# The first four tiles: output-projection and key blocks interleaved over six PSUM banks, K/V/R weights fetched two groups ahead, first tile reordered

## The chip, the cores and the metric

One Trainium2 chip, all 8 cores. Each core runs the same program on one batch row of 8192 tokens; no core waits for another. The metric is the device time of the slowest core in microseconds. The engines of a core are TensorE (PE; its weight loads are listed as PEld), VectorE (DVE), ScalarE (ACT), GpSimd (POOL) and SyncE (SP). POOL and SP only issue transfers here; every engine works through its own list of instructions in order and waits on semaphores.

## The reference

One layer: an RWKV block (time mixing, then channel mixing) beside a feed-forward block with ternary weights, on the same normalized input.

```python
xn = _layernorm(x)                                   # over 1024 features
# RWKV block on xn
h  = _ln(xn); h1 = _time_shift(h)
k, v, r = mix(h, h1, tm_mix_*) @ tm_Wk, tm_Wv, tm_Wr # three 1024x1024 products
x1 = xn + (sigmoid(r) * _wkv(k, v, w, u)) @ Wo       # decay recurrence over time
h  = _ln(x1); h1 = _time_shift(h)
kc = square(relu(mix(h, h1, cm_mix_k) @ cm_Wk))      # 1024 -> 4096
rc = sigmoid(mix(h, h1, cm_mix_r) @ cm_Wr)
x2 = x1 + rc * (kc @ cm_Wv)                          # 4096 -> 1024
# feed-forward block on xn
f  = gelu(xn @ ternary(W1).T + b1) @ ternary(W2).T + b2
return x + x2 + f
```

## The kernel before

**Layout.** Features lie on the partitions (8 chunks of 128), tokens on the free axis, in 16 tiles of 512 tokens. A "block" is one output chunk of one product: eight 128x128 by 128x512 matmuls into one PSUM bank (`block`, L326). All matrix work is such blocks; two more blocks with a matrix of ones give the sums of a normalization.

**Order.** The program is written out by Python into one list per engine (`Streams.put`, L47, which also drops waits that the engine has already passed). The feed-forward part of a tile runs four tiles later (`LAG`): the loop at L910 over tiles 0 to 3 has attention and channel mixing only, since the ternary weights are being made meanwhile; the loop at L947 over the other tiles has both. The change edits the first loop, what lies ahead of it, and a few helpers.

In a tile t of the first loop TensorE does, in this order: the eight output-projection blocks (`wo_stage`, L746), two blocks of sums (`ln2_stats`), for t above 0 the last five chunks of the value product of tile t-1 (`value_part`, 20 blocks), and then `channel_stage` (L861): 32 key blocks, the receptance blocks and the first three value chunks (all eight in tile 3). Between these blocks `between()` counts n and puts in one K/V/R group of tile t+1 (`kvr_group`, L578: three blocks into banks 5, 6 and 7) every 5 blocks from n = 16 in tile 0, every 5 from n = 11 in tiles 1 and 2, every 7 from n = 11 in tile 3.

**The rest is in lanes.** `Lanes` (L64) holds Python generators, each step of which emits a few DVE or ACT instructions with an estimated cost. `advance`, called after each block, gives 0.93 of the block's 1740 ns to the lanes in order of priority; `drain` emits all that is left of a lane at once. The lanes are `wkv` (the recurrence of one group, priority 1), `ln2_apply` (second normalization and mixing of this tile, pair by pair of chunks into xk2 and xr2, priority 0), `ln0_stats`, `ln0_mix` and `ln0_norm` (first normalizations of the next tile, its mixing into xk, xv and xr, and its store to memory). `ln0_mix` stops while `mixer["hold"]` is set, which `ln2_stats` sets after its two blocks, and `ln2_apply` clears. A K/V/R group of tile t+1 needs the whole `ln0_mix(t+1)`, an output-projection block the whole att, a key block the whole xk2.

**Evictions.** A key block is evicted by ACT in two instructions (Relu at L796, Square at L798) from banks 2, 3 and 4 in turn; output-projection blocks by DVE (L758) from banks 2 to 7.

**Weights.** In tile 0, and for some of the value rows in tile 1, they come as f32 through POOL with a conversion to bf16 (`prepare`, L280) into one of two slots of ring A (K/V/R rows), four of ring B or two of ring C, and SP writes each row back to memory (the z tensors) as soon as it has landed. From then on SP loads the bf16 rows (`fetch`). SP works in order: a load stands behind all write-backs issued before it. A slot is refilled when `release` is told the last matmul that read it. From tile 1 a paced lane (`tern_run`) also reads W1 and W2 through POOL, sums and rounds them on ACT and clips them on DVE.

Of the kernel before, what the change touches and what calls it, by code (L numbers as in the profile page):

```python
# [15 lines left out]
E = 1024  # L16
# [112 lines left out]
def build_program(t_total=T_TOTAL):  # L129
# [207 lines left out]

    short = {"banks": [2, 3, 4, 5, 6, 7], "at": 0}
# [10 lines left out]
    def ln0_stats(j):  # L349
# [31 lines left out]
        for c in range(EC):  # L381
# [4 lines left out]
        a1 = ACT(lambda s_: s_.activation(out=R0[:], in_=pb[bk2][:], func=AF.Ln, scale=1.0 / E, bias=LN0_EPS),  # L386
                 t6, tk.get("ln0_done"), tk.get("norm_done"))
        a2 = ACT(lambda s_: s_.activation(out=R01[:], in_=pb[bk2][:], func=AF.Ln, scale=(1.0 + LN_EPS) / E,
                                          bias=LN0_EPS * LN_EPS))
        bank_free[bk2] = [a2]  # L390
        ACT(lambda s_: s_.activation(out=R0[:], in_=R0[:], func=AF.Exp, scale=-0.5), a1)
        tk[f"rstd{j}"] = ACT(lambda s_: s_.activation(out=R01[:], in_=R01[:], func=AF.Exp, scale=-0.5), a2)
# [67 lines left out]
    def ln0_norm(j):  # L460

        cur = xn[j % 2]
        for p in range(4):
            tn = DVE(lambda v, p=p: v.tensor_mul(pair(cur, p), pair(x, p), twice(R0)),
                     tk[f"rstd{j}"], tk.get(f"x2_free{j % 2}"))
# [14 lines left out]
    def ln2_apply(t, s1, s2, bk1, bk2):  # L480
# [14 lines left out]
        for p in range(5):  # L495
# [22 lines left out]
    def wkv(t, g, kb, vb, rb, ktok, vtok, rtok):  # L518
# [47 lines left out]
        def last():  # L566
            wk["nd_free"] = tk["att"] = DVE(lambda v: v.tensor_mul(ck(att, g), ND[:, 0, :], ND[:, 1, :]), l2,  # L567
# [10 lines left out]
    def kvr_group(t, g):  # L578
        unit = fetch("wkvr", g)
        if t == 1 and g + 1 < EC:  # L580
            prefetch("wkvr", g + 1)
# [8 lines left out]
        release(unit, toks[-1])  # L590
        tk["kvr_done"] = toks[-1]
# [154 lines left out]
    def wo_stage(t):  # L746
        short["banks"], short["at"] = [2, 3, 4, 5, 6, 7], 0
        cur = xn[t % 2]
        unit = None
        ev = None  # L750
        for c in range(EC):
            if c % 2 == 0:
                unit = fetch("wo", c // 2)
            bk = short_bank()
            tok = block(bk, unit[0], (c % 2) * 1024, [ck(att, k) for k in range(8)], True, True, unit[1], tk["att"])
# [4 lines left out]
            if c % 2:  # L760
# [3 lines left out]
                    ev, tk.get("w1_done"), tk.get("cwk_done"))  # L764
            ln.advance(BLOCK_NS, 750.0)
# [23 lines left out]

    def cwk_block(m, unit):  # L790
        bk = short_bank()
        tok = block(bk, unit[0], (m % 2) * 1024, [ck(xk2, k) for k in range(8)], True, True, unit[1], tk["mix2"])
        if m % 2:
            release(unit, tok)
        i = m % 2
# [65 lines left out]
    def channel_stage(t, chunks, first, every, hooks):  # L861
# [12 lines left out]
        for m in range(FC):  # L874
# [25 lines left out]
    for g in range(EC):  # L900
# [4 lines left out]
        if g == 4:  # L905
            lane_s = ln.start(3, ln0_stats(1))
    refill(rC)


    for t in range(LAG):  # L910
        ln.drain(wkv_lanes[-1])
        ln.drain(lane_s)
# [5 lines left out]
        ev, s = wo_stage(t)  # L918
# [11 lines left out]
        def mixed(t=t, lane=mix_lanes[0]):  # L930
            if t == 0:
                prefetch("wkvr", 0)
# [10 lines left out]
        gates = channel_stage(t, range(EC if t == LAG - 1 else EC - LATE), first, every, hooks)  # L943
# [155 lines left out]
```

How the kernel before makes its waits and increments, by code:

```python
            def body(eng):  # L981
                for ws, fn, sem, by in st.ops[name]:
                    for s, v in ws:
                        eng.wait_ge(sems[s], v)
                    ins = fn(eng)
                    if sem is not None:
                        ins.then_inc(sems[sem], by)
```

## Time and profile before

| | us |
|---|---|
| median of 3 runs | 5135.28 |
| lowest, highest | 5126.62, 5996.21 |
| the profiled execution | 5128.33 |
| span of its slowest core (core 0, the one shown) | 5126.5 |
| spans of its other cores | 5105.4 to 5123.9 |
| TensorE busy | 4776.4 (93%) |
| VectorE, ScalarE busy | 2595.4, 2131.2 |

The highest of the three runs lies 17% above the others. All rows below are of core 0 of the profiled execution, and their times count from its first instruction.

### The profile page before, as it was taken

The page shows a single profiled execution, that of the slowest core. Times are in us where ns is not written, and L with a number is a line of the kernel's source. Part 1 is how long each engine was busy: PE and PEld are TensorE (multiplying, and loading weights), DVE is VectorE, ACT ScalarE, POOL GpSimd, SP SyncE. Part 2 cuts the span into 40 slices and gives each one's busy share as a digit, 9 for nine tenths or more (in the row PEclk, how much of TensorE's full clock was granted, in tenths as well). Part 3 has the DMA queues.
Part 4 walks back from the last instruction along what each step waited for, and adds up shares of the span by engine and source line. Part 5 has one row for each costly group of instructions (what it writes and reads, how often), then busy time and mean ns, then how long its engine had stood idle before and what let it go on. Part 6 is the DMA issues. An engine that isn't in the chain of part 4 may idle for free.

```text
span 5126.5 us, 63290 instructions; the slowest of 8 cores (5105.4 to 5126.5 us)
## 1 busy us (share of the span) xinstructions
PE 4776.4 (93%) x21484; PEld 2154.9 (42%) x21922; DVE 2595.4 (51%) x3424; ACT 2131.2 (42%) x3436; POOL 429.7 (8%) x807
## 2 busy tenths in 40 slices
PE   3577888799999999999999999999999999999999
PEld 1233333344444444444444444444444444444444
DVE  6746566666555545555554555545555554330111
ACT  2433756554544434354443435444343544342111
POOL 0000111122000000100000010000001000000111
PEclk8789999899999999999999999999999999999999
DMA  6477878899455564645556464555646455555765
GB/s 159 103 193 180 261 230 244 249 291 318 165 189 199 177 225 160 231 158 192 202 179 216 163 230 163 192 190 196 202 166 226 159 185 192 175 185 189 230 227 179
DMA packets 273339, 1021.40 MB, mean 199 GB/s; under 512 B 34432, under 2 KB 34560, under 8 KB 267008
## 3 DMA queue, kind: packets, MB, share of 16 engines
q1 hardware_dynamic: 194112, 706.83, 40.6%
q0 software_dynamic: 78768, 310.43, 20.7%
q8 instruction: 183, 3.00, 0.2%
q14 instruction: 132, 1.08, 0.1%
q10 hardware_dynamic: 144, 0.07, 0.0%
HBM read 916.52 MB, written 127.93 MB: 204 GB/s over the span
## 4 chain that ended last, share of the span: by engine, by line
PE 84%; DMA 7%; DVE 4%; issue 2%; ACT 2%; POOL 0%; another core or an unknown queue 0%; DVEq 0%; SPq 0%; ACTq 0%; POOLq 0%
PE pb L333 82%; DMA rb<-w2t 2%; DMA rb<-w1t 1%; DMA ra<-zwkvr 1%; PE pb L382 1%; PE pb L775 1%; DMA rb<-cwk 1%; DMA zw2t<-XC 1%; PE pb L779 1%; DVE xr L419 1%; DVE TT L414 0%; DMA x<-xS 0%; DVE xk L419 0%; DMA rb<-cwv 0%; ACT TT L376 0%
## 5 line engine op out<-in xcount | busy, mean ns | idle before, releaser
L333 PE MATMUL pb<-xk,rb 128*128 128x512 bf16 x8028 | 1785.6, 381 | 81.5 <-DVE xr L419 60.0
L333 PE MATMUL pb<-big,rb 128*128 128x512 bf16 x8034 | 1792.3, 379 | 16.9 <-DMA rb<-cwv 5.7
L333 PEld LDWEIGHTS pb<-xk,rb 128*128 128x128 bf16 x8192 | 802.7, 98 | 1051.9 <-issue 96.5
L333 PEld LDWEIGHTS pb<-big,rb 128*128 128x128 bf16 x8192 | 801.9, 98 | 979.2 <-issue 16.4
L796 ACT ACTIVATE RC<-pb 128x512 f32<-128x512 f32 x512 | 301.4, 589 | 725.5 <-PE pb L333 640.3
L703 ACT ACTIVATE big<-pb,vecs_s 128x512 bf16<-128x512 f32 x512 | 346.3, 686 | 563.9 <-PE pb L333 550.3
L735 DVE SCALAR_TENSOR_TENSOR RO<-pb,vecs_s,RO 128x512 f32<-128x512 f32 x128 | 95.9, 749 | 580.3 <-PE pb L333 386.2
L333 PE MATMUL pb<-xk,ra 128*128 128x512 bf16 x1005 | 255.6, 396 | 109.9 <-DMA ra<-zwkvr 44.8
L525 DVE TENSOR_TENSOR_SCAN W<-wdec,carry,pb 128x512 f32<-128x512 f32 x128 | 163.7, 1279 | 361.4 <-PE pb L333 361.4
L798 ACT ACTIVATE big<-RC 128x512 bf16<-128x512 f32 x512 | 322.5, 630 | 47.5 <-ACT RC L796 0.8
L838 DVE TENSOR_TENSOR RO<-pb,RC 128x512 f32<-128x512 f32 x113 | 77.9, 690 | 478.1 <-PE pb L333 478.1
L758 DVE TENSOR_TENSOR xn<-xn,pb 128x512 bf16<-128x512 bf16 x128 | 87.6, 687 | 411.2 <-PE pb L333 362.7
L406 ACT ACTIVATE hp<-TT,vecs_s 128x512 bf16<-128x512 f32 x256 | 194.4, 809 | 163.6 <-DVE TT L501 148.0
L333 PE MATMUL pb<-att,rb 128*128 128x512 bf16 x1006 | 227.5, 384 | 37.0 <-DVE att L567 34.8
L333 PE MATMUL pb<-xr,rc 128*128 128x512 bf16 x997 | 243.6, 385 | 15.2 <-DMA rc<-cwr 7.6
L814 ACT ACTIVATE RC<-pb 128x512 f32<-128x512 f32 x128 | 76.2, 595 | 421.3 <-PE pb L333 363.6
L333 PE MATMUL pb<-xv,ra 128*128 128x512 bf16 x1000 | 244.4, 385 | 4.8 <-DVE W L543 3.9
L543 DVE TENSOR_TENSOR W<-W,pb 128x512 f32<-128x512 f32 x128 | 88.0, 687 | 317.6 <-ACT W L536 310.9
L333 PE MATMUL pb<-xr,ra 128*128 128x512 bf16 x1001 | 240.2, 379 | 1.4
L536 ACT ACTIVATE W<-W 128x1024 f32<-128x1024 f32 x128 | 134.1, 1048 | 174.7 <-DVE W L533 174.7
L333 PEld LDWEIGHTS pb<-xk,ra 128*128 128x128 bf16 x1024 | 102.0, 100 | 241.2 <-issue 130.1
L419 DVE SCALAR_TENSOR_TENSOR xk<-TT,vecs_s,hp 128x512 bf16<-128x512 f32 x256 | 182.0, 747 | 11.9 <-DVE TT L414 0.9
(102 smaller groups left out, 3875.6 us busy)
## 6 DMA issues: line engine op xcount, KB each, us to landing
rb<-zw1t SPq DMA_DIRECT2D x256, 512.0 KB, 3.7
rb<-zw2t SPq DMA_DIRECT2D x256, 512.0 KB, 5.0
rb<-zcwk SPq DMA_DIRECT2D x240, 512.0 KB, 4.9
rb<-zcwv SPq DMA_DIRECT2D x240, 512.0 KB, 6.0
ra<-zwkvr SPq DMA_DIRECT2D x120, 768.0 KB, 7.2
resS<-RO POOLq DMA_DIRECT2D x128, 256.0 KB, 5.7
rb<-w1t POOLq DMA_DIRECT2D x64, 512.0 KB, 8.9
rb<-w2t POOLq DMA_DIRECT2D x64, 512.0 KB, 10.1
```

The costliest lines, as they stand in the source:

```text
L333: tok = PE(lambda t, k=k: t.matmul(pb[bank][:], slot[:, col + k * 128:col + (k + 1) * 128], rhs[k], start=start and k == 0, stop=stop and ...
L406: a1 = ACT(lambda s, c=c: s.activation(out=h[:, c, 1:NT + 1], in_=src[:, c, :], func=AF.Identity, scale=cv[gname][:, 2 * p + c:2 * p + c + 1],
L419: m = DVE(lambda v, c=c, mname=mname, dst=dst: v.scalar_tensor_tensor(out=ck(dst, 2 * p + c), in0=tc[:, c, :], scalar=cv[mname][:, 2 * p + ...
L525: p = DVE(lambda v: v.tensor_tensor_scan(out=W4[:, 0, now], data0=w_b, data1=pb[kb][:], initial=carry[:, g, 0:1], op0=ALU.add, op1=ALU.max ...
L536: ex = ACT(lambda s: s.activation(out=W4[:, 2:4, now], in_=W4[:, 2:4, now], func=AF.Exp), d0, d1)
L543: bv = DVE(lambda v: v.tensor_mul(W4[:, 1, now], W4[:, 2, now], pb[vb][:]), ex, vtok)
L703: gel[m] = ACT(lambda s, m=m, bk=bk: s.activation(out=ck(big, m), in_=pb[bk][:], func=AF.Gelu, bias=cv["b1f"][:, m:m + 1]), tok, *big_free ...
L735: e1 = DVE(lambda v, r=r, c=c, bk=bk: v.scalar_tensor_tensor(out=RO[r][:], in0=pb[bk][:], scalar=cv["b2f"][:, c:c + 1], in1=RO[r][:], op0= ...
L758: ev = DVE(lambda v, c=c, bk=bk: v.tensor_add(ck(cur, c), ck(cur, c), pb[bk][:]), tok, xn_st[t])
L796: a1 = ACT(lambda s, i=i, bk=bk: s.activation(out=RC[i][:], in_=pb[bk][:], func=AF.Relu), tok, rl_free[i])
L798: sqr[m] = ACT(lambda s, i=i, m=m: s.activation(out=ck(big, m), in_=RC[i][:], func=AF.Square), a1, *big_free[m // 8])
L838: e1 = DVE(lambda v, r=r: v.tensor_mul(RO[r][:], pb[bk][:], gate), tok, a3, ro_free[r])
```

## The change

It touches only what the first loop and the code ahead of it emit, but for one swap in `ln0_stats` that every tile has.

```diff
@@ prepare: every f32 row load also waits for the first tile's x
-        ready = dma("gpsimd", f"G{ring.name}{i}", slot[:], wdram[w][rows, :], *ring.free[i])
+        ready = dma("gpsimd", f"G{ring.name}{i}", slot[:], wdram[w][rows, :], *ring.free[i], *x_in[0])
@@ new
+    def rounds(jobs, parts):
+
+        done = {}
+        for at, (ks, ready) in enumerate(parts):
+            for bank, slot, col, rhs, loaded in jobs:
+                for k in ks:
+                    w = [ready] if k == ks[0] else []
+                    if at == 0 and k == ks[0]:
+                        w += [loaded, *bank_free[bank]]
+                    tok = PE(lambda t, bank=bank, slot=slot, col=col, rhs=rhs, k=k: t.matmul(
+                        pb[bank][:], slot[:, col + k * 128:col + (k + 1) * 128], rhs[k], start=k == 0, stop=k == 7),
+                        w, inc=k == 7)
+                done[bank] = tok
+        return done
@@ ln0_stats: R01 (for mixing) complete first, then R0 (for the store), each with its own token
+        for r, key, scale, eps in ((R01, "rstd", (1.0 + LN_EPS) / E, LN0_EPS * LN_EPS), (R0, "rstd0", 1.0 / E, LN0_EPS)):
...
@@ ln0_norm
+        while f"rstd0{j}" not in tk:
+            yield -2000.0
@@ ln2_apply, after the mixing of each pair
+                tk[f"mix2_{pend[3]}"] = tk["mixed"]
@@ wkv: one token for each group's slice of att
-            wk["nd_free"] = tk["att"] = DVE(lambda v: v.tensor_mul(ck(att, g), ND[:, 0, :], ND[:, 1, :]), l2,
+            wk["nd_free"] = tk[f"att{g}"] = DVE(lambda v: v.tensor_mul(ck(att, g), ND[:, 0, :], ND[:, 1, :]), l2,
@@ kvr_group
-        if t == 1 and g + 1 < EC:
-            prefetch("wkvr", g + 1)
...
         release(unit, toks[-1])
+        if t == 1 and g + 2 < EC:
+            prefetch("wkvr", g + 2)
@@ wo_stage(t, split): six blocks side by side, k 0 to 6 once att6 is there, k 7 with att7
+        if split:
+            for r in range(3):
+                units[r] = fetch("wo", r)
+            early = rounds([(2 + c, units[c // 2][0], (c % 2) * 1024, rhs, units[c // 2][1]) for c in range(6)],
+                           [(range(7), tk["att6"]), ((7,), tk["att7"])])
...
+            if split and c == 3:
+                mixer["hold"] = True
@@ new: the first six key blocks, two k's of each as each pair of xk2 is there
+    def cwk_first():
+
+        units = [fetch("cwk", r) for r in range(3)]
+        done = rounds([(2 + m, units[m // 2][0], (m % 2) * 1024, [ck(xk2, k) for k in range(8)], units[m // 2][1])
+                       for m in range(6)], [((2 * p, 2 * p + 1), tk[f"mix2_{p}"]) for p in range(4)])
+        for m in range(6):
+            if m % 2:
+                release(units[m // 2], done[2 + m])
+            cwk_evict(m, 2 + m, done[2 + m])
@@ channel_stage(..., split)
-        for m in range(FC):
+        if split:
+            cwk_first()
+            n = 6
+        for m in range(n, FC):
@@ ahead of the first loop
-        if g == 4:
-            lane_s = ln.start(3, ln0_stats(1))
     refill(rC)
+    prefetch("wkvr", 0)
+    prefetch("wkvr", 1)
@@ the first loop
-        ln.drain(lane_s)
+        if t:
+            ln.drain(lane_s)
...
-        ev, s = wo_stage(t)
+        ev, s = wo_stage(t, True)
...
-            mix_lanes[:] = [ln.start(2, ln0_mix(t + 1))]
+            mix_lanes[:] = [ln.start(2, itertools.chain(ln0_stats(1), ln0_mix(1)))]
...
-        first, every = (16, 5) if t == 0 else (11, 5) if t < LAG - 1 else (11, 7)
...
-            if t == 0:
-                prefetch("wkvr", 0)
...
+        first, every = (16, 4) if t == 0 else (12, 4) if t < LAG - 1 else (12, 6)
```

The statistics of tile 1 thus move from between the K/V/R groups of tile 0 to behind the second normalization of tile 0. In the second loop `wo_stage` and `channel_stage` are called as before.

## Rows read from the trace of the kernel before

**Rows 1.** The page, parts 1 and 2: busy us (share) xinstructions; TensorE in 40 slices

```profile
PE 4776.4 (93%) x21484; PEld 2154.9 (42%) x21922; DVE 2595.4 (51%) x3424; ACT 2131.2 (42%) x3436; POOL 429.7 (8%) x807
...
PE   3577888799999999999999999999999999999999
```

**Rows 2.** Windows of core 0: stretch, length, busy us (instructions) by engine, granted clock, DMA share, GB/s

```profile
144.50:172.00 27.50, 5.17 (x12) 1.69 (x12) 17.36 (x20) 8.44 (x11) 0.00 (x0) 0.57 0.00 0
...
190.50:217.70 27.20, 0.00 (x0) 0.01 (x1) 25.84 (x30) 8.70 (x18) 0.00 (x0) 0.59 0.22 68
...
269.40:407.70 138.30, 112.75 (x480) 49.41 (x490) 69.83 (x94) 58.59 (x93) 10.60 (x20) 0.91 0.69 174
407.70:421.30 13.60, 0.00 (x0) 0.02 (x1) 10.46 (x15) 2.80 (x4) 0.54 (x1) 0.61 0.17 58
...
514.77:646.86 132.09, 118.89 (x520) 52.22 (x529) 78.23 (x106) 96.27 (x166) 15.34 (x29) 0.97 0.86 254
646.86:660.30 13.44, 0.00 (x0) 0.01 (x1) 4.05 (x8) 2.30 (x4) 2.67 (x5) 0.60 0.51 176
...
986.67:1152.66 165.99, 154.87 (x678) 68.33 (x692) 103.16 (x147) 95.13 (x134) 35.34 (x66) 0.97 0.91 282
1152.66:5126.50 3973.84, 3933.48 (x17911) 1789.48 (x18275) 1857.74 (x2440) 1565.75 (x2513) 290.32 (x542) 1.00 0.58 195
```

**Rows 3.** Timeline, VectorE, start: start, length, what, [idle before <-releaser]

```profile
23.23 1.23 DVE L354 TENSOR_TENSOR TT<-x 128x1024 f32<-128x1024 f32 x1 [12.66 <-DMA x<-xS]
```

**Rows 4.** Timeline, TensorE, first tile: statistics, and the first key block

```profile
160.10 2.04 PE L362 MATMUL pb<-TT,ones_f 128*128 128x512 f32 x2 [15.60 <-DVE TT L358]
...
217.72 3.15 PE L333 MATMUL pb<-xk,rb 128*128 128x512 bf16 x7 [27.23 <-DVE xr L419]
```

**Rows 5.** Timeline, VectorE, first tile: att slices of groups 6 and 7

```profile
146.60 0.68 DVE L567 TENSOR_TENSOR att<-ND 128x512 bf16<-128x512 f32 x1
...
154.87 0.69 DVE L567 TENSOR_TENSOR att<-ND 128x512 bf16<-128x512 f32 x1 [1.54 <-ACT ND L564]
```

**Rows 6.** Timeline, SyncE queue, first tile: write-backs ahead of the first K/V/R load

```profile
181.21 82.14 SPq L232 DMA_DIRECT2D zcwk<-rb  x12
```

**Rows 7.** Timeline, TensorE, channel stage of the first tile: waits for weights

```profile
269.41 3.57 PE L333 MATMUL pb<-xk,ra 128*128 128x512 bf16 x8 [21.38 <-DMA ra<-zwkvr]
...
314.03 0.59 PE L333 MATMUL pb<-xk,ra 128*128 128x512 bf16 x1 [14.56 <-DMA ra<-zwkvr]
...
348.10 5.80 PE L333 MATMUL pb<-xr,rc 128*128 128x512 bf16 x16 [7.58 <-DMA rc<-cwr]
```

**Rows 8.** Timeline, VectorE: mixing for the second tile

```profile
234.99 1.42 DVE L419 SCALAR_TENSOR_TENSOR xk<-TT,vecs_s,hp 128x512 bf16<-128x512 f32 x2
...
241.43 1.41 DVE L419 SCALAR_TENSOR_TENSOR xk<-TT,vecs_s,hp 128x512 bf16<-128x512 f32 x2
...
250.20 1.41 DVE L419 SCALAR_TENSOR_TENSOR xr<-TT,vecs_s,hp 128x512 bf16<-128x512 f32 x2
```

**Rows 9.** Timeline, VectorE, around the second tile's second normalization

```profile
448.04 0.68 DVE L487 SCALAR_TENSOR_TENSOR R<-pb,R 128x512 f32<-128x512 f32 x1
...
484.66 0.69 DVE L838 TENSOR_TENSOR RO<-pb,GG 128x512 f32<-128x512 f32 x1 [4.87 <-remote]
...
490.90 1.41 DVE L419 SCALAR_TENSOR_TENSOR xr<-TT,vecs_s,hp 128x512 bf16<-128x512 f32 x2
```

**Rows 10.** Timeline, TensorE: K/V/R groups of tiles 2 and 4; key blocks of tile 3

```profile
514.77 1.89 PE L333 MATMUL pb<-xk,ra 128*128 128x512 bf16 x8
...
957.60 18.62 PE L333 MATMUL pb<-xk,rb 128*128 128x512 bf16 x71 [16.61 <-DVE xr L419]
...
986.67 3.57 PE L333 MATMUL pb<-xk,ra 128*128 128x512 bf16 x8 [6.38 <-DVE xr L419]
```

**Rows 11.** The page, part 5: evictions of the key blocks on ScalarE

```profile
L796 ACT ACTIVATE RC<-pb 128x512 f32<-128x512 f32 x512 | 301.4, 589 | 725.5 <-PE pb L333 640.3
...
L798 ACT ACTIVATE big<-RC 128x512 bf16<-128x512 f32 x512 | 322.5, 630 | 47.5 <-ACT RC L796 0.8
```

More of the change, by code:

```diff
@@ L1 @@
+import itertools
 import numpy as np
@@ L385, in ln0_stats @@
         tk["sq_free"] = t6
[L386 to L392, printed above, removed]
+        for r, key, scale, eps in ((R01, "rstd", (1.0 + LN_EPS) / E, LN0_EPS * LN_EPS), (R0, "rstd0", 1.0 / E, LN0_EPS)):
+            a1 = ACT(lambda s_, r=r, scale=scale, eps=eps: s_.activation(
+                out=r[:], in_=pb[bk2][:], func=AF.Ln, scale=scale, bias=eps),
+                t6, tk.get("ln0_done"), tk.get("norm_done"))
+            tk[f"{key}{j}"] = ACT(lambda s_, r=r: s_.activation(out=r[:], in_=r[:], func=AF.Exp, scale=-0.5), a1)
+        bank_free[bk2] = [a1]
     hp_free = [None, None]
@@ L744, in w2_stage, with wo_stage @@
             ln.advance(BLOCK_NS, 1550.0)
-    def wo_stage(t):
+    def wo_stage(t, split=False):
         short["banks"], short["at"] = [2, 3, 4, 5, 6, 7], 0
         cur = xn[t % 2]
-        unit = None
-        ev = None
+        rhs = [ck(att, k) for k in range(8)]
+        units, early = {}, {}
+        if split:
[3 more added lines that the diff above has]
+                           [(range(7), tk["att6"]), ((7,), tk["att7"])])
         for c in range(EC):
-            if c % 2 == 0:
-                unit = fetch("wo", c // 2)
+            if c % 2 == 0 and c // 2 not in units:
+                units[c // 2] = fetch("wo", c // 2)
+            unit = units[c // 2]
             bk = short_bank()
-            tok = block(bk, unit[0], (c % 2) * 1024, [ck(att, k) for k in range(8)], True, True, unit[1], tk["att"])
+            if c in (0, 1, 2, 3, 4, 5) and split:
+                tok = early[bk]
+            else:
+                tok = block(bk, unit[0], (c % 2) * 1024, rhs, True, True, unit[1], tk["att7"])
             if c % 2:
@@ L794, in cwk_block, with cwk_evict @@
             release(unit, tok)
+        cwk_evict(m, bk, tok)
+    def cwk_evict(m, bk, tok):
         i = m % 2
@@ L859, in value_part, with channel_stage @@
                 cwv_block(t, c, q, unit, rc)
-    def channel_stage(t, chunks, first, every, hooks):
+    def channel_stage(t, chunks, first, every, hooks, split=False):
         short["banks"], short["at"] = [2, 3, 4], 0
@@ L925, in build_program, with mixed @@
         if t == 0:
-            mix_lanes[:] = [ln.start(2, ln0_mix(t + 1))]
+            mix_lanes[:] = [ln.start(2, itertools.chain(ln0_stats(1), ln0_mix(1)))]
         lane_n = ln.start(2, ln0_norm(t + 1))
-        first, every = (16, 5) if t == 0 else (11, 5) if t < LAG - 1 else (11, 7)
-        def mixed(t=t, lane=mix_lanes[0]):
-            if t == 0:
-                prefetch("wkvr", 0)
+        first, every = (16, 4) if t == 0 else (12, 4) if t < LAG - 1 else (12, 6)
+        def mixed(lane=mix_lanes[0]):
             ln.drain(lane)
@@ L942, in build_program @@
         hooks = {first: mixed, first + 4: normed, first + 16: stats}
-        gates = channel_stage(t, range(EC if t == LAG - 1 else EC - LATE), first, every, hooks)
+        gates = channel_stage(t, range(EC if t == LAG - 1 else EC - LATE), first, every, hooks, True)
     finish_lanes()
```

2 lines of the change are left out of this document (1 added, 1 removed).

## The prediction

> **What bounds the kernel now.** I read the slices of the page first: TensorE is at nine tenths or more from the tenth slice on and well below it only in the first nine [rows 1]. Then the windows by stretch. From 1152.66 us to the end, 3973.84 us hold by my count of the code some 2280 blocks, 1.74 us a block, at clock 1.00 [rows 2]. That part is bound by TensorE, the change leaves its order alone, and I give it nothing. All there is to win lies ahead of 1152.66: of the 4776.4 us busy [rows 1] 842.9 lie there, so TensorE waits 310 us, and runs now and then at the lower of its two clocks.
>
> Where do these waits sit? In each of the four tiles the same ring closes: the K/V/R groups feed the recurrence on VectorE, the last slice of att frees the output projection, its result goes through normalization and mixing on VectorE, mixing frees the key blocks and the next K/V/R groups. The rows to look at are those in which TensorE does nothing at all: 27.2 us of the second normalization of tile 0, then 13.60 and 13.44 us before the output projections of tiles 1 and 2, and some 22 of the 27.5 us ahead of the projection of tile 0 [rows 2]. Beside them stand waits for weights in tile 0 of 21.38, 14.56 and 7.58 us [rows 7].
>
> **The change part by part.** Sums are made against the profiled execution, 5128.33 us for a span of 5126.5; the median of the runs shown is 7 us above it. E0, E1, E2 are the ends of the channel stages of tiles 0, 1 and 2, before at 407.7, 646.9 and 873.6.
>
> *Start.* The second half of the first x is added at 23.23, after 12.66 us of waiting for its transfer, which shares the engines with six converted weight rows [rows 3]. Held back, those rows leave it the engines. It can't start adding before 10.6, where the wait began; landing by 11.5 gives 12 us (bounds 10 and 12.7). The weights then land some 10 us later, but are read only after statistics and four pairs of mixing at 6.44 us each [rows 8]: nothing. The swap in the statistics frees mixing two ACT instructions of some 0.6 us sooner [by rows 11]: 1 us. Sum 13.
>
> *Tile 0, att to the sums.* Before, TensorE's K/V/R groups end at 144.5, tile 1's statistics take 15.60 us of waiting and more [rows 2, 4], att is whole at 155.56 [rows 5], and the second sum ends at 190.5. After, 42 matmuls (7 k of six banks) start with att6 at 147.3 [rows 5]; at 1.74/8 = 0.22 us each that is 9.1, plus some 2 at the low clock (eight matmuls after a wait took 3.57 us against 1.89 without one [rows 7, 10]): 158.5. Six matmuls on att7 and two blocks, 4.8, to 163.3; the last add, square and second sum, some 4.5: 168. Gain 22 (19 to 25).
>
> *Tile 0, key blocks against mixing.* The 27.2 us on VectorE stay. Only 12 of 48 matmuls are left behind the last pair instead of 48, 7.9 us less. But the next K/V/R group needs tile 1's mixing, and this now has the statistics ahead of it. From the end of the second mixing I count: sums on VectorE 4.5; the small matmul and the copy behind seven evictions of 0.59 + 0.63 [rows 11], to 10; four subtractions to 15; squares behind evictions to 21; sums and the two logarithms and exponentials to 26; three store steps fill the wait for the first pair, then four pairs at 6.44 apart [rows 8], to 55 to 58. Before, the group started 51.8 us after that point, 217.6 to 269.41 [rows 4, 7], held by its weights although mixing had ended at 251.6 [rows 8]. So the wait for weights goes and a wait for VectorE stands in its place: loss 5 (from a gain of 2 to a loss of 12). The 7.9 us are gone in it; TensorE idles some 28 us there.
>
> *Tile 0, the other groups.* The write-backs issued ahead of the first K/V/R loads hold SP's queue for 82.14 us [rows 6]. Two groups ahead, each load stands behind write-backs of rows that are needed before it anyway. Its new price, SP waiting for the last matmul of a group, holds up only write-backs and loads of later rows. I take 13 of the 14.56 us [rows 7] and leave the receptance wait of 7.58, whose two slots are as before; 0 if converted rows are late instead, 17 with everything. So E0 comes 13 + 22 - 5 + 13 = 43 us earlier.
>
> *Tile 1.* The groups every four blocks end six blocks sooner against the end of the stage, 10 us, and 9 us of matmuls run before the last slice of att: the 13.60 goes. Six blocks side by side also leave one add, not eight, behind the last, but the converted rows of the value part start later; I count 57.7 us from E0 to the end of the value part against 76.6 (407.7 to 484.3): gain 19. The hold moved to the fourth block takes two pairs of `ln0_mix` (until 448.04) out of the way of the normalization [rows 9]. The gap of 8.2 after the value part, up to the last pair at 492.3 [rows 9], is then filled. But all four pairs of tile 2's mixing now come behind it. ACT has twelve evictions of 1.22 us [rows 11], some five passes of the ternary sums and four pairs' scalings from 8 us on, which ends near 37, and the last pair's mixing 5 later: the first group starts 42 us after the value part, before 30.5 (484.3 to 514.77 [rows 10]): loss 11.5. The rest, 132.09 us before [rows 2], has one block less and fewer waits for evictions: 127. Sum 12.5.
>
> *Tile 2* is the same with value rows that arrive as bf16 before and after: 13.44 us of waiting goes [rows 2], less at the edges: 9.5.
>
> *Tile 3.* The part from E2 to the end of its value part takes 55.5 instead of 67.4: gain 12. From there (941.0) the first group came 45.7 us later, with 16.61 us of waiting for the normalization, then two pairs, the last waited for for 6.38 [rows 10]; with four pairs, but a normalization that starts 11 sooner and no clips emitted while a lane is drained, 48: loss 2 to 3. The rest, 165.99 [rows 2], falls to 161. Sum 14.
>
> Total 43 + 12.5 + 9.5 + 14 = 79, and 5128.3 - 79 = 5049; **I forecast 5050 us**, 1.6% under the median.
>
> *A rule against the change.* The bursts of twelve matmuls between pairs come after waits of some 4 us, and eight matmuls took 3.57 us after a wait [rows 7], so a burst may take 5 us and not 2.6. The Trainium skill (TensorE: Matmul & The Clock Gate, section HAM oscillation) says that bursts parted by waits each start at the low clock, and advises to keep one output's K tiles together; the trace agrees on the price of a start. By the rule the bursts before the last pair cost nothing, since TensorE is idle there anyway, and the last costs 2.6 us in tile 0, which the wait for mixing swallows: 0 in the sum. By it, too, each idle stretch that the change removes saves 1.7 us; I count that within the terms.
>
> **The rivals.**
>
> *A. Mixing is no new wait.* If VectorE and ACT run the four pairs beside the key blocks faster than counted, the losses of 5, 11.5, 11.5 and 2.5 vanish and the filled gaps count: the sum rises by 31 to 110, and to 180 if TensorE waited nowhere but for receptance weights. For it: VectorE is free a third of the time in these stretches, 78.23 of 132.09 us busy [rows 2]. Against: four pairs at 6.44 are 26 us, and they can't begin before the first two key evictions. Times 5018 and 4950; I give 0.24 to all gains above 100.
>
> *B. Transfers take over.* DMA engines are at 0.86 and 0.91 in the later stretches of tiles 1 and 3 [rows 2]. If the denser order only meets later rows, the 13 of tile 0 and some 5 to 8 in each other tile go: gain 40 to 50, 5083. Against: at 0.69 in tile 0 [rows 2] there is room. 0.19.
>
> *C. The early parts aren't early.* If att6 is multiplied only just before att7, or the pairs of the key input come together, the rounds save nothing. In tile 0, 10 us go; in the others the denser groups cover most: gain 65, 5063. Against: 7.6 us lie between the two slices [rows 5]. 0.07.
>
> *D. Slower, by the deferred mixing.* In tile 3 VectorE waits for ACT in front of each clip, and two pairs took from 957.6 to 986.67, 29 us [rows 10]. If all four pairs go at that pace in tiles 1 to 3, they end 57 us after the normalization. In tiles 1 and 2 that is 61 behind the value part, 30 later than before, against 24 won elsewhere: 6 lost each. In tile 3 it is 65 against 45.7, with 17 won: 2 lost. Tile 0's four pairs, stretched by 0.6, cost 16 of its 43, and the weights' 13 go too: 14 left. The sum is 0 there; beyond that pace each further microsecond a pair costs 16, and one gives 5144. Against: `drain` emits no clips, and tiles 0 and 1 have none. 0.06.
>
> **How the numbers follow.** Forecast (gain 55 to 100) 0.44, A 0.24, B 0.19, C 0.07, D 0.06. The range runs from 5005, inside A, to 5092, the weak end of B, where the bounds of the terms in tile 0 (together 25 either way) also end; it leaves out some 0.1 on each side. Its own range for the forecast is 5030 to 5073. A change of over 2% is 103 us, about what a measurement of this kernel can tell from none: faster is A but for its edge and a little of the forecast, 0.27; slower by over 2% is the far end of D, 0.02; 0.71 lies within.
>
> **What will show it.** In the trace after: the second addition near 11; no statistics between tile 0's groups; output-projection matmuls before the last att multiply in all four tiles; key matmuls in four bursts in tile 0; the first K/V/R group of each next tile waiting for the last mixing on VectorE (28 us in tile 0, some 15 in tiles 1 and 2) and not for weights; no wait of 13 us ahead of projections; the steady part again 3974 us. I am wrong low if these first groups start without a wait, wrong high if waits for converted rows or for evictions grow between the groups, or if the last slice of att comes later than 9 us after a channel stage ends.

## The result and the profile after

| | before | after |
|---|---|---|
| profiled execution, us | 5128.33 | 5054.1 |
| spans of the eight cores in it | 5105.4 to 5126.5 | 5035.6 to 5052.5 |
| ratio after / before, 95% interval | | 0.9873, 0.9855 to 0.989 |

The change saves 1.3%, some 65 us: clear of noise, but less than 2%. The medians of all runs are 5126.34 and 5166.77, since in half of the six runs after, as in many others here, the four cores of one die ran at a lower granted clock and took longer; such cores are left out of every ratio, table and comparison of this document.

The page of the changed kernel: busy times, then TensorE in 40 slices.

```profile
PE 4804.2 (95%) x21922; PEld 2154.2 (43%) x21922; DVE 2593.8 (51%) x3424; ACT 2133.8 (42%) x3436; POOL 430.0 (9%) x807
...
PE   4598988899999999999999999999999999999999
```

Each slice is 126 us. Against [rows 1] TensorE is below nine tenths in six slices, not in eight, and none but the first two is under eight tenths, where three more stood at seven. The windows of core 5, the slowest here, give the shape; the columns are those of [rows 2].

```profile
125.20:138.33 13.13, 7.40 (x33) 2.92 (x32) 11.80 (x18) 4.81 (x7) 0.00 (x0) 1.00 0.85 235
212.90:241.22 28.32, 0.21 (x2) 0.03 (x1) 27.80 (x35) 9.58 (x19) 0.53 (x1) 0.57 0.58 150
241.22:364.17 122.95, 112.78 (x490) 49.20 (x491) 79.17 (x108) 61.61 (x98) 10.61 (x20) 0.93 0.77 193
364.17:430.32 66.15, 55.68 (x241) 23.73 (x239) 41.68 (x52) 15.52 (x27) 8.07 (x15) 0.92 0.82 197
430.32:467.32 37.00, 23.19 (x96) 9.49 (x97) 25.72 (x33) 24.84 (x49) 4.75 (x9) 0.89 0.86 275
467.32:587.89 120.57, 116.76 (x523) 51.56 (x523) 80.72 (x110) 91.68 (x158) 14.82 (x28) 0.98 0.82 260
1077.42:5052.50 3975.08, 3952.04 (x18277) 1788.60 (x18275) 1857.66 (x2440) 1568.13 (x2512) 290.59 (x542) 1.00 0.59 195
```

Three things answer to [rows 2]. The stretch without a matmul is now before the first K/V/R group of tile 1 (212.9 to 241.22), with VectorE busy 27.80 of 28.32 us. From that group to the end of tile 0's channel stage it takes 122.95 us where it took 138.30. And from the end of the first loop on, 3975.08 us stand against 3973.84: the rest of the kernel is as it was.

The single rows of TensorE on core 5 of the changed kernel, tile 0 first:

```profile
138.33 12.21 PE L348 MATMUL pb<-att,rb 128*128 128x512 bf16 x48 [4.44 <-DVE att L585]
...
168.92 4.50 PE L348 MATMUL pb<-xk,rb 128*128 128x512 bf16 x12 [10.28 <-DVE xr L434]
175.26 2.75 PE L348 MATMUL pb<-xk,rb 128*128 128x512 bf16 x12 [1.83 <-DVE xr L434]
181.70 7.04 PE L348 MATMUL pb<-xk,rb 128*128 128x512 bf16 x24 [3.69 <-DVE xr L434]
...
241.22 3.34 PE L334 MATMUL pb<-xk,ra 128*128 128x512 bf16 x8 [28.11 <-DVE xr L434]
...
282.80 3.57 PE L334 MATMUL pb<-xk,ra 128*128 128x512 bf16 x8 [3.71 <-DMA ra<-zwkvr]
...
311.82 3.57 PE L334 MATMUL pb<-xr,rc 128*128 128x512 bf16 x8 [5.31 <-DMA rc<-cwr]
...
364.17 10.52 PE L348 MATMUL pb<-att,rb 128*128 128x512 bf16 x48
...
384.88 3.18 PE L804 MATMUL pb<-xn,ones_bf 128*128 128x512 bf16 x8 [6.64 <-DVE xn L785]
...
455.81 7.01 PE L334 MATMUL pb<-xk,rb 128*128 128x512 bf16 x24 [6.82 <-ACT RC L838]
...
467.32 3.57 PE L334 MATMUL pb<-xk,ra 128*128 128x512 bf16 x8 [4.51 <-DVE xr L434]
```

L348 is the new `rounds`. At 168.92, 175.26 and 181.70 are the bursts of the first key blocks, the last two run together (24 matmuls in 7.04 us, where 48 stood behind the last pair before and 12 were forecast). The waits of 21.38 and 14.56 us for K/V/R rows [rows 7] are gone, but for 3.71; the receptance row still makes TensorE wait 5.31 at 311.82, before 7.58. The projection of tile 1 begins at 364.17 with no wait, in place of the 13.60 [rows 2]. New are the 6.64 us before the sums (384.88) and the 6.82 before a key block (455.81).

To see where in the first loop the time is won, one core is not enough: the cores end it up to 24 us apart before, 21 us after. So here and below stand medians over the eight cores of one profiled execution: the starts, read from the timelines, of the projection of each tile ("Wo"), of the first K/V/R group behind it ("first K"), and the end of the first loop.

| | Wo 0 | first K 1 | Wo 1 | first K 2 | Wo 2 | first K 3 | Wo 3 | first K 4 | end |
|---|---|---|---|---|---|---|---|---|---|
| before | 174.2 | 273.9 | 422.0 | 516.9 | 658.8 | 745.6 | 878.7 | 979.4 | 1140.8 |
| after | 138.0 | 239.6 | 361.3 | 466.1 | 586.7 | 685.0 | 806.6 | 906.8 | 1068.7 |
| earlier by | 36.2 | 34.3 | 60.7 | 50.8 | 72.1 | 60.6 | 72.1 | 72.6 | 72.1 |

A pattern shows: the gain stands at the projection of tiles 1 and 2, and the next first K/V/R group has given 10 and 11.5 us of it back. It is won again in the groups behind. After the projection of tile 2 the medians show nothing more won.

### The profile page after: what moved, and what is told of

Same layout as the page of the kernel before. It is cut to its first block, busy times and chain, and to the rows that moved or that the text cites. A ratio compares the mean times of both kernels' runs of the same rounds, so it can differ in the third digit from the quotient of the medians.

```text
span 5052.5 us, 63792 instructions; the slowest of 8 cores (5035.6 to 5052.5 us)
## 1 busy us (share of the span) xinstructions
PE 4804.2 (95%) x21922; PEld 2154.2 (43%) x21922; DVE 2593.8 (51%) x3424; ACT 2133.8 (42%) x3436; POOL 430.0 (9%) x807
## 4 chain that ended last, share of the span: by engine, by line
PE 89%; DMA 4%; DVE 3%; issue 2%; ACT 2%; POOL 0%; DVEq 0%; SPq 0%; ACTq 0%; POOLq 0%
PE pb L334 85%; PE pb L348 1%; DMA rb<-w2t 1%; PE pb L804 1%; PE pb L398 1%; PE pb L808 1%; DVE xr L434 0%; DMA ra<-wkvr 0%; DVE TT L429 0%; DMA ra<-zwkvr 0%; DVE xn L785 0%; DMA rb<-cwk 0%; DMA rb<-zcwk 0%; DMA rb<-cwv 0%; ACT RC L838 0%
## 5 line engine op out<-in xcount | busy, mean ns | idle before, releaser
L334 PE MATMUL pb<-xk,rb 128*128 128x512 bf16 x8000 | 1752.5, 380 | 35.1 <-ACT RC L838 32.2
L334 PEld LDWEIGHTS pb<-xk,rb 128*128 128x128 bf16 x8000 | 783.9, 98 | 989.3 <-issue 54.4
L334 PE MATMUL pb<-xr,rc 128*128 128x512 bf16 x1024 | 244.3, 383 | 12.6 <-DMA rc<-cwr 5.9
L434 DVE SCALAR_TENSOR_TENSOR xk<-TT,vecs_s,hp 128x512 bf16<-128x512 f32 x256 | 182.1, 747 | 11.5 <-DVE TT L429 0.5
L334 PE MATMUL pb<-att,rb 128*128 128x512 bf16 x832 | 182.3, 379 | 3.0 <-DMA rb<-zwo 2.9
```

Of the source, the lines that this page charges most:

```text
L334: tok = PE(lambda t, k=k: t.matmul(pb[bank][:], slot[:, col + k * 128:col + (k + 1) * 128], rhs[k], start=start and k == 0, stop=stop and ...
L434: m = DVE(lambda v, c=c, mname=mname, dst=dst: v.scalar_tensor_tensor(out=ck(dst, 2 * p + c), in0=tc[:, c, :], scalar=cv[mname][:, 2 * p + ...
```

## The experiments

Each is an edit of the changed kernel, but for "The pace alone". "End" is the end of the first loop as above, beside 1068.7; it is read from the one execution that was profiled. How far one execution carries is seen from a second measure, the *core span*: the median span of the four cores of a die, and of these the median over the dies of all executions. It is 5107.4 us before (18 dies, from the executions beside the last three experiments; 5108.5 from those beside other experiments) and 5040.8 after (9 dies, 5033.7 to 5058.5). A few microseconds are therefore not told from none. Both measures of every run stand in a table under *Shares* below.

**The mixing held sooner.** In `wo_stage` the hold is set ahead of the loop.

```diff
+        if split: mixer["hold"] = True
         for c in range(EC):
...
-            if split and c == 3:
-                mixer["hold"] = True
```

> Mixing of the next tile is held from the first projection block on, not from the fourth. Theory (the 6.6 to 7.2 us of waiting before the sums of tiles 1 to 3 come from mixing instructions that stand among the adds in VectorE's queue): these waits fall to about 1 us each, 18 us in all; the mixing that is moved, some 6 us a tile, comes back as a wait before the first K/V/R group (tile 2: 4.5 grows to about 5, tiles 3 and 4: up to 6 more), so the first loop ends 5 to 12 us earlier than in the changed kernel. Rival (VectorE is late for another reason, att or the clips): the waits before the sums stay above 5 us and the end doesn't move.

Measured on cores 4 to 7, beside the same four of the changed kernel. Medians: first K at 238.5, 471.5, 695.9 and 921.6, end 1078.0, against 242.0, 466.3, 684.6, 909.5 and 1070.6. That is 7 us later (14 by core span), where 5 to 12 earlier was expected. TensorE, core 5:

```profile
375.24 1.89 PE L803 MATMUL pb<-xn,ones_bf 128*128 128x512 bf16 x8 [0.94 <-DVE xn L786]
...
397.89 9.90 PE L334 MATMUL pb<-big,rb 128*128 128x512 bf16 x32 [3.80 <-DMA rb<-cwv]
...
458.24 7.03 PE L334 MATMUL pb<-xk,rb 128*128 128x512 bf16 x24 [6.81 <-ACT RC L837]
...
476.21 3.57 PE L334 MATMUL pb<-xk,ra 128*128 128x512 bf16 x8 [10.94 <-DVE xr L434]
```

What the new wait hangs on is shown for tile 1: without mixing between the adds it falls from 6.64 to 0.94. The price was wrong, sign included. In tile 1 the earlier sums win nothing, since the value part then waits for its converted rows (3.80 us in one place), and the mixing moved behind it costs more there: 10.94 us of waiting instead of 4.51, and some 11 and 16 before the first groups of tiles 3 and 4. (In tile 3 the stretch up to the end of the value part gets 8 us shorter, and the one behind it 13 longer.) VectorE's adds of the changed kernel, core 5, show why mixing here is cheap:

```profile
365.92 0.69 DVE L585 TENSOR_TENSOR att<-ND 128x512 bf16<-128x512 f32 x1
373.79 0.69 DVE L785 TENSOR_TENSOR xn<-xn,pb 128x512 bf16<-128x512 bf16 x1 [7.19 <-PE pb L348]
374.40 1.22 DVE L460 TENSOR_TENSOR TT<-x,R 128x1024 f32<-128x1024 f32 x1
375.53 1.88 DVE L785 TENSOR_TENSOR xn<-xn,pb 128x512 bf16<-128x512 bf16 x3
...
380.88 0.74 DVE L434 SCALAR_TENSOR_TENSOR xv<-TT,vecs_s,hp 128x512 bf16<-128x512 f32 x1
381.54 0.68 DVE L785 TENSOR_TENSOR xn<-xn,pb 128x512 bf16<-128x512 bf16 x1
382.14 0.74 DVE L434 SCALAR_TENSOR_TENSOR xv<-TT,vecs_s,hp 128x512 bf16<-128x512 f32 x1
...
384.06 0.68 DVE L785 TENSOR_TENSOR xn<-xn,pb 128x512 bf16<-128x512 bf16 x1
```

After the last slice of att VectorE waits 7.19 us for the first six blocks to end, then has all adds at once, with mixing among them (L460, L434), and is done with them at 384.7, where the last block ended at 378.2.

**The mixing held later.** The two lines at the fourth block are left out, so that `ln2_stats` sets the hold, as in the kernel before.

> Mixing of the next tile is held only after the two sum blocks, as in the kernel before; all else as changed. By median over the cores the changed kernel begins the first K/V/R groups of tiles 2, 3, 4 at 466, 685, 907 and ends the first loop at 1069; holding from the first block on gave 476, 700, 928 and 1086. Theory (mixing done during the projection is nearly free, since VectorE and ScalarE wait there for TensorE, while behind the value part it stands in ScalarE's full queue): a later hold does another pair early and gives 5 us or more in each of tiles 1 to 3, the loop ends near 1055, although the wait before the sums stays or grows. Rival (the fourth block is the best place, both ends lose): it ends at 1069 or later.

Measured: 238.9, 460.9, 680.0 and 896.9, end 1059.0. The waits before the sums stay (6.0 to 7.2), those for mixing before the first groups of tiles 2, 3 and 4 are 0.0 on every core. 5 us are won by the first group of tile 2, none more by that of tile 3, and 10 by that of tile 4 and at the end (7 by core span): the theory holds in its direction, but not with 5 us in each tile, and it stays short of the 1055. (The 476, 700, 928 and 1086 of the expectation are the first experiment's medians over all eight cores; with cores 4 to 7 alone the order stays the same.)

**ScalarE relieved of the ternary sums.**

```diff
-                lambda ...: s.activation(out=tout[o][:], in_=tin[i][:], func=AF.Abs,
+                lambda ...: s.activation(out=tout[o][:, 0:128], in_=tin[i][:, 0:128], func=AF.Abs,
```

> Leaves out seven eighths of each ternary sum on ScalarE (only the first 128 of 1024 columns are summed, so the scale of the ternary weights is another one); the transfers stay. Theory (behind the value parts of tiles 1 and 2 ScalarE is full: twelve evictions, five sums and the scaling of four pairs, and this sets the first K/V/R group): the wait of 6.8 us for a key eviction falls below 3, and the first groups of tiles 2 and 3 come 4 us or more sooner against the start of their key blocks. Rival (VectorE's four pairs alone set it): the first groups move by less than 1.5 us.

Measured: 240.1, 463.5, 676.0 and 895.2, end 1056.7. TensorE, core 5:

```profile
449.15 7.32 PE L334 MATMUL pb<-xk,rb 128*128 128x512 bf16 x24 [5.01 <-ACT RC L838]
459.92 3.51 PE L334 MATMUL pb<-xk,ra 128*128 128x512 bf16 x8 [3.45 <-DVE xr L434]
```

Neither side is right as stated. The wait for an eviction fell only from 6.82 to 5.01. Against the start of their key blocks, the measure of the expectation, the first groups of tiles 2 and 3 come 3.6 and 3.4 us sooner (37.0 to 33.4, 36.0 to 32.7), just short of its 4; from the sums on, the stretches shrank by 1.3 us (84.1 to 82.8) and 3.4 (77.6 to 74.2), and the whole loop by 12 (core span 9). ScalarE's queue costs something all along; that it alone sets the first group is not borne out. What the eviction waits for is settled by "Key blocks one after the other" below.

**Statistics of tile 1 where they were.** The lane starts at g == 4 again and is drained ahead of tile 0's projection.

> The statistics of tile 1 are back among the K/V/R groups of tile 0; all else as changed. Theory (TensorE idles 28 us before the first K/V/R group of tile 1 because statistics and mixing stand in a row behind the second normalization, so moving the statistics only moved the wait): the projection of tile 0 starts some 15 us later, the first group of tile 1 at about the same time, within 5 us of 241. Rival (moving the statistics is what tile 0 gained): the first group comes 15 us or more later, and the whole kernel is 15 slower than the changed one.

Measured: projection at 162.1, first group at 237.8, end 1070.8; ratio to before 0.986 (0.9735 to 0.9985). TensorE waits 15.54 us for the statistics again, on core 5 at 150.61, and for the first group 4.52 in place of 28.11:

```profile
150.61 2.05 PE L378 MATMUL pb<-TT,ones_f 128*128 128x512 f32 x2 [15.54 <-DVE TT L374]
...
238.22 3.52 PE L334 MATMUL pb<-xk,ra 128*128 128x512 bf16 x8 [4.52 <-DVE xr L434]
```

So this part of the change moved 24 us of waiting from one place to another and won at most little: 2 us by the end of the loop, 8 by core span.

**The start undone.** `*x_in[0]` is dropped from `prepare`.

> The weight rows don't wait for x. Theory: x's second half lands 11 us later, near 23, everything behind it shifts by 11 to 12 us and the first loop ends that much later than in the changed kernel. Rival (the later tiles absorb a shift at the start, since their transfers are spread further): less than 6 us are left at the end of the first loop.

Measured: first group of tile 0 at 67.2 instead of 56.2, of tile 1 at 249.9, end 1083.6; ratio 0.9877 (0.975 to 1.0004). VectorE adds the second half of x on core 5 at 22.86 after 11.95 us of waiting, in the changed kernel at 12.07 after 0.70:

```profile
22.86 1.23 DVE L370 TENSOR_TENSOR TT<-x 128x1024 f32<-128x1024 f32 x1 [11.95 <-DMA x<-xS]
```

10 to 11 us are this part's, and none of them is absorbed; what goes beyond them in the 15 at the end (14 by core span) lies within what executions differ.

**Projections one after the other.** In `wo_stage` the `if split:` ahead of `rounds` is `if False:`; the hold stays.

> Projection blocks one after the other again, each waiting for the whole att; the hold at the fourth block stays. Theory: in tile 0 the projection starts near 146 instead of 138 and ends later by 6 to 9 us; in tiles 1 to 3 att is ready when the stage begins (its last slice came at or before the end), so there the side-by-side order saves nothing there, and since its adds bunch up behind the mixing it costs 5 us a tile: undone, tiles 1 to 3 gain 10 to 15 us, and the first loop ends within 5 us of the changed kernel's 1077. Rival (the early blocks pay in every tile): it ends 20 us or more later.

Measured: Wo 145.8, first K 249.9, 477.8, 692.3, 905.9, end 1065.2; ratio 0.9837 (0.9754 to 0.9921). (The 1077 of the expectation is core 5's end; here it ends at 1078.5.) At the first groups the kernel is behind by 10 us (tile 1), 12 (tile 2) and 7 (tile 3), then ahead by 1, and by 3 or 4 at the end: the plain order costs 10 in tile 0 and 1 to 2 in tile 1, and wins it back later, most of it in tile 3 (from that projection to the end of the loop 251.6 us instead of 261.2, medians of the single cores' lengths). The side-by-side projection pays in tile 0 alone, where TensorE would wait 7.86 us for att (core 5) and now works in that time. Over the whole kernel the two orders can't be told apart (core spans 5042.1 and 5040.8).

With blocks one after the other the waits before the sums fall to 1.1 us in tiles 1 and 3, but in tile 2 the wait stays at 6.1. Core 5 in tile 2, first TensorE, then VectorE:

```profile
625.87 3.57 PE L804 MATMUL pb<-xn,ones_bf 128*128 128x512 bf16 x8 [6.37 <-DVE xn L785]
...
618.86 1.22 DVE L429 TENSOR_TENSOR TT<-hp 128x1024 f32<-128x1024 bf16 x1 [6.06 <-ACT hlast L424]
```

Here VectorE stands 6.06 us at a mixing instruction whose scaling ScalarE has not done yet, and the last five adds stand behind it in its list.

**Key blocks one after the other.** `cwk_first` is replaced by six `cwk_block` calls.

> The first six key blocks come one after the other in banks 2, 3, 4 and wait for the whole second mixing. Theory (in tile 0 what they save goes into the wait of 28 us before the first K/V/R group; in tiles 1 and 2 the second mixing is nearly over when the value part ends, and the six evictions at once fill ScalarE's queue): tile 0's first group comes within 3 us of 240, with some 20 us of waiting instead of 28, and the first loop ends within 6 us of 1069. Rival (the side-by-side key blocks are worth their 7.8 us a tile in tiles 1 to 3): it ends 15 us or more later.

Measured: first K 245.0, 467.5, 681.7, 909.9, end 1072.0; ratio 0.9879 (0.9855 to 0.9902). The theory holds at the end, and its picture of tile 0 doesn't: the first group comes 5.5 later and still waits 28.62 us on core 5. By my reading of the code the statistics are placed by blocks passed and so move with them; no run parts this from other causes:

```profile
186.99 14.50 PE L334 MATMUL pb<-xk,rb 128*128 128x512 bf16 x56 [27.24 <-DVE xr L434]
...
249.04 3.57 PE L334 MATMUL pb<-xk,ra 128*128 128x512 bf16 x8 [28.62 <-DVE xr L434]
...
463.85 7.07 PE L334 MATMUL pb<-xk,rb 128*128 128x512 bf16 x32 [1.34 <-ACT RC L838]
```

The last row is from tile 1: where the changed kernel waits 6.82 us for an eviction, the longest such wait ahead of the first K/V/R group is now 1.34 (at most 2.3 on any core, and under 1.0 in tiles 2 and 3). So that wait comes from the six evictions that fall due at once. In its place the waits for mixing are back: 4.46 us in tile 1, 7.97 in tile 2 and 12.43 in tile 3 before the first key block, and 5.66 instead of 4.51 before the first group of tile 2. So the bundle moves the wait to the next engine more than it removes it, which fits how little it costs to undo it (3 us at the end, 6 by core span).

**The old pace.** `first, every` is (16, 5), (12, 5), (12, 7).

> K/V/R groups every 5, 5 and 7 blocks again, the first ones where the change puts them. Theory (the closer pace is what lets the last slice of att be ready when the channel stage ends): the last slice comes up to 10 us later against the end of the stage, so a wait appears before or within the projection in tiles 1 and 2, of about 4 us (the rest is covered by the seven eighths of the early blocks), and the first loop ends 5 to 15 us later. Rival (the early blocks alone cover it): within 3 us.

Measured: Wo 1 at 366.4, first K 2 478.9, Wo 2 602.2, first K 3 706.3, first K 4 937.5, end 1093.0; ratio 0.9925 (0.9908 to 0.9943). 24 us (26 by core span), more than expected, and not by the way expected. The wait for att is 5.2 in tile 1 and nil in tile 2. Instead the recurrence takes the lanes' time of the projection, mixing doesn't get started before it is held (the wait before tile 1's sums is 0.94, as with the mixing held sooner), and the first group waits 10.5 us in tile 2 and 15.0 in tile 4, as there.

**One group ahead.** The old prefetch calls.

> K/V/R rows of tile 1 one group ahead again, the first from the hook at the first group. Theory (tile 0 no longer has room: 28 us of waiting before the first group cover the first load, but the later loads stand behind write-backs): the first group comes within 3 us of 240, the later groups of tile 1 wait 10 to 15 us for their rows, and the first loop ends 8 to 15 us later than 1069. Rival (the transfers have time anyway): within 3 us.

Measured: first K 1 at 238.4, Wo 1 375.7, end 1078.3; ratio 0.9888 (0.9856 to 0.9921). Up to the first group nothing changes, then

```profile
275.90 3.31 PE L334 MATMUL pb<-xk,ra 128*128 128x512 bf16 x8 [12.51 <-DMA ra<-zwkvr]
```

The theory holds: 10 us by the end of the loop; by core span, 5058.7 beside 5040.8, it is 18.

**The pace alone**, in the kernel before.

```diff
-        first, every = (16, 5) if t == 0 else (11, 5) if t < LAG - 1 else (11, 7)
+        first, every = (16, 4) if t == 0 else (12, 4) if t < LAG - 1 else (12, 6)
```

> The kernel before with nothing changed but the places of the K/V/R groups, which are those of the changed kernel (every 4, 4 and 6 blocks, the first at 12 in tiles 1 to 3). Theory (the pace is the largest single part: undone, it cost the changed kernel 24 us): the first loop ends 15 to 30 us before the 1141 of the kernel before, by shorter waits for att. Rival (the pace only pays with the rows fetched two groups ahead and the early blocks): less than 8 us.

Cores 0 to 3 alone are read. They end the loop at 1093.4, 1125.2, 1122.2 and 1094.8, in the kernel before at 1152.7, 1137.6, 1137.0 and 1150.0: 35 us by the means. That is one pair of executions, and the one of the kernel before was a late one (its dies stand at 5119.0 and 5115.4, the core span over all executions at 5107.4). By core span the edit gives 17 us (5090.7, 7 dies): one line has about a quarter of what the whole change gives, and the theory's 15 to 30 hold. The way is the one expected; the wait for att before tile 1's projection falls from 13.60 to 2.41 (core 1):

```profile
416.98 13.29 PE L333 MATMUL pb<-att,rb 128*128 128x512 bf16 x53 [2.41 <-DVE att L567]
```

**Late hold, side by side in tile 0 only.** An edit of the changed kernel again: the hold as in the second experiment, and `wo_stage(t, t == 0)`.

> The late hold, and the projection blocks side by side in tile 0 only. By median over the cores the changed kernel ends the first loop at 1069, with the late hold alone at 1059, with plain projections everywhere at 1065 (10 us lost in tile 0, the rest won back later). Theory (both add up, since side by side costs in tiles 1 to 3 and pays in tile 0): the first loop ends at 1045 to 1053 and the kernel is 20 us or more faster than the changed one. Rival (the late hold already takes what plain projections win, by mixing between the adds): it ends at 1055 to 1062.

Measured: first K 238.7, 457.6, 677.7, 886.2, end 1048.5: 20 us before the changed kernel, as the theory had it (17 by core span, 5023.5). The ratio to before is 0.9828 (0.9791 to 0.9865), the lowest of all: faster than the kernel before by 1.4 to 2.1%. Against the changed kernel the loop says 20 us, while the intervals of the two ratios still overlap a little (0.9865 over 0.9855). The wait before the sums is 0.94 in tile 1 and 1.14 in tile 3 with a late hold, since plain projections give VectorE its adds one by one; in tile 2 it is 6.8, as with plain projections above. Core 1, tile 1:

```profile
358.52 15.66 PE L334 MATMUL pb<-att,rb 128*128 128x512 bf16 x64 [2.52 <-DVE att L585]
375.13 1.89 PE L802 MATMUL pb<-xn,ones_bf 128*128 128x512 bf16 x8 [0.94 <-DVE xn L785]
```

## Why the prediction was right, and where not

The time, 5054.1 for a forecast of 5050, and the place of the change's work were right; several terms were wrong and cancelled, which is luck. The gain is less close than the time: 74 us between the two profiled executions, but 65 by the ratio and 67 by core span, for a forecast of 79. The 74 are high because the execution before, from which the sum starts, was a late one (see "The pace alone").

*Start*, 13 forecast: on core 5 x is added at 12.07, the first K/V/R group comes 12.6 us earlier by median. Right, and undone it costs 11 there, 14 by core span.

*Tile 0.* The group after it came at 241.22 with 28.11 us of waiting for VectorE, for 28 forecast, and the stage ended at 364.17 for a forecast of 364.7 (407.7 less 43). The statement that the statistics' wait only changes place was tested by putting them back: the first group moved by 2 us. The weights' 13 are 10 by the loop of their own experiment and 18 by core span. Three of the rows of bursts also settle the clock: the first took 4.50 us for twelve matmuls after 10.28 of waiting (granted clock 0.60 in that stretch), the second 2.75 after 1.83 (1.00), and 24 took 7.04 after 3.69 (0.75; 0.29 us each, where 0.22 is full speed). So after the short wait the clock hadn't fallen at all, and the last burst lost under 2 us to the low clock, which the waiting for mixing swallowed. The Trainium skill (TensorE: Matmul & The Clock Gate, section HAM oscillation) advises against such parted bursts; the rows agree on the price of a start for the first and the third burst and not for the second, and to go against the advice cost nothing here.

*Tiles 1 to 3, the step that failed.* "Six blocks side by side also leave one add, not eight, behind the last" was wrong. They leave all the adds at once, and mixing that was not yet held stands among them: 6.6, 6.6 and 7.2 us before the sums, 20 in all, where I had the time of one add, 0.7 us. It takes both in tiles 1 and 3: with no mixing there the waits are 0.9 and 1.8 us, with the blocks one after the other 1.1 and 1.1. In tile 2 the bundle isn't needed for it: with plain blocks the wait is still 6.1 us (even in the kernel before, with only the pace changed, 6.4 on core 1), by mixing that waits for ScalarE; with no mixing the first sum waits 0.9, but the second then 4 to 5 for ScalarE. I also took the hold at the fourth block for one that keeps all mixing out; the lane gets in before. So from a stage's end to the end of the value part it took 66.1 us in tile 1 instead of 57.7 (6.6 of it before the sums, 3.8 for converted rows). Against this the first group came 37.0 us behind the value part and not 42, since part of its mixing was done by then (with all four pairs behind, in the first experiment, it is 47.7), and the rest of the tile took 120.6 and not 127. Thus tile 1's sum came out near the 12.5 by three errors that cancel.

*The sum by tile.* From stage end to stage end it depends on the cores that are compared. On the slowest ones (core 0 before, core 5 after), for which the forecast was summed, start and tile 0 gave 43.5 us (43 forecast), tile 1 15.5 (12.5), tile 2 0.3 (9.5), tile 3 16.0 (14): 75 for 79. By the medians above, with the old waits for att of 13.6, 12.8 and 7.3 us counted into the tiles that they open, it is 47.1, 12.2, 5.5 and 7.3: 72. Either way start, tile 0 and tile 1 stand, and tile 2 was sized too high. There the wait of 12.8 us is gone, but 5.0 of it came back before the sums (6.6 for 1.6), and the wait for mixing before the key blocks turned into one of 6.8 for an eviction. Of tile 3 one can't say: it took 266 to 279 us on the cores before, 258 to 266 after. Its sums come 21.2 us behind the start of the projection and not 17.1, by the adds above.

*Rivals.* A's premise, that mixing is no wait, is false in tile 0 (28 us) and only seemingly true in tile 2: its next group, first K 3, starts without a wait, but the key block ahead of it waits 6.81 us on core 5 for an eviction. B didn't come: with the denser groups the DMA share in tile 0 rose from 0.69 [rows 2] to 0.77 and the waits for rows still shrank. C is half true, by another mechanism: in tiles 2 and 3 the last att slice is there before the stage ends (no waits in either kind of projection), so the early start has nothing to win. D's stretch to 57 us wasn't seen: all pairs held back cost 11 to 16 us of waiting, and 7 at the end of the loop.

In the details two readings of mine were a little off: the slices of the page [rows 1] reach nine tenths from the ninth on, not the tenth, and 5050 lies 1.7% under the median, not 1.6%.

*Shares.* End of the first loop in the profiled execution, and core span over all executions, in us; the last two columns are differences from the changed kernel. For the mixing held sooner the end is read on cores 4 to 7 and set beside their 1070.6, for the pace alone it is the mean of cores 0 to 3, beside 1144.3 before.

| | end | core span (dies) | by end | by span |
|---|---|---|---|---|
| before | 1140.8 | 5107.4 (18) | +72 | +67 |
| changed | 1068.7 | 5040.8 (9) | | |
| old pace | 1093.0 | 5067.0 (9) | +24 | +26 |
| one group ahead | 1078.3 | 5058.7 (7) | +10 | +18 |
| start undone | 1083.6 | 5055.2 (6) | +15 | +14 |
| statistics where they were | 1070.8 | 5048.6 (7) | +2 | +8 |
| key blocks one after the other | 1072.0 | 5047.2 (6) | +3 | +6 |
| projections one after the other | 1065.2 | 5042.1 (7) | -3 | +1 |
| mixing held later | 1059.0 | 5033.9 (5) | -10 | -7 |
| mixing held sooner | 1078.0 | 5054.4 (3) | +7 | +14 |
| short ternary sums | 1056.7 | 5031.8 (2) | -12 | -9 |
| late hold, side by side in tile 0 only | 1048.5 | 5023.5 (10) | -20 | -17 |
| pace alone, in the kernel before | 1108.9 | 5090.7 (7) | | +50 |

The seven parts undone one at a time (old pace to mixing held later) add up to 41 of 72 by the ends and to 66 of 67 by core span. The dies of one kernel scatter by several microseconds (5033.7 to 5058.5 in the changed one), so a term under some 6 us is not told from none, and the close sum is no proof that the parts don't act on each other: the projection bursts are worth 10 us in tile 0 and cost about as much in tile 3, and the pace is worth 26 on top of the rest and 17 alone. The swap in the statistics was not tested by itself, and why the cores part by 20 us is open.

## What to carry to other kernels

Where engines close a ring, a wait that is removed comes back at the next engine that was hidden behind it; so ask of each idle place what could run there for nothing before moving work away from it (VectorE's idle 7 us by the projection were the best place for the mixing). Work that is bundled to fill a wait also bundles its evictions, and they queue behind whatever else the other engine was given meanwhile. Try the one-line parts of a change by themselves: the spacing of the groups alone did 17 us where the whole change did 67. And check what a single pair of executions says against the spans of all: for that line the pair said 35 of 72.

## What the runs showed of the hardware

Two cores that are neighbours by number end the same program at different times, in alternation. In the profiled execution of the last experiment, the fastest kernel here, spans and granted clocks of the cores:

```profile
core 0: 5033.0 us, clock 0.981
core 1: 5015.7 us, clock 0.986
core 2: 5038.0 us, clock 0.980
core 3: 5016.8 us, clock 0.985
...
```

One of each pair is 17 to 25 us faster, and in other executions it is the other one (core 0 at 5012.6 and core 1 at 5038.4 us in the next). All of it arises in the first loop (ends at 1060.1 and 1036.4 on cores 0 and 1). In the changed kernel that loop is where the DMA engines are busiest (shares of 0.77 to 0.86 on core 5 from 241.22 to 587.89, 0.59 behind the loop). That the two share something in memory is a guess; no run here tests it.
